# A router's last product made straight in token layout, inside a planned five-engine pipeline

## What is computed

```
x = x + layernorm(mamba(layernorm(x)))     # gated state-space block: in-projection, 4-tap causal
                                           # convolution, SiLU, softplus(delta), scan of 16 states
                                           # over 512 tokens for 512 channels, gate, out-projection
x = x + layernorm(experts(layernorm(x)))
experts(x):  Q = x WQ', K = x WK'; two branches (forward, inverse), each
   xV = Q V[k], yW = cumsum_t(K W[k]) for k in 8 experts of rank 64
   h = gelu(Q_side W1' + b1);  logits = h W2' + b2 + expert_bias;  w = softmax(logits)   # 8 logits a token
   out = sum_k (xV * yW * w[k]) U[k] + w b, over the number of tokens so far
   result = (forward + alpha inverse) WO'
```

## Time and profile before

| | us |
|---|---|
| three runs | 2418.75, 2423.53, 2423.81 |
| median | 2423.53 |
| the profiled execution | 2417.08 |
| its span, from the first to the last instruction | 2415.1 |
| VectorE busy | 2173.3 |
| TensorE busy | 2128.0 |
| GpSimd busy | 1854.3 |
| ScalarE busy | 1842.0 |
| mean granted clock of TensorE | 0.953 |

### The profile page before, as it was taken

One profiled execution on the slowest core, in us unless ns is written; L12 is line 12 of the kernel. 1 busy time (PEld: TensorE's weight loads), 2 busy tenths in 40 slices (PEclk: granted clock), 3 DMA queues, 4 the chain that ended last, 5 costly groups with the idle time before them and its releaser, 6 DMA issues.

```text
span 2415.1 us, 35863 instructions
## 1 busy us (share of the span) xinstructions
PE 2128.0 (88%) x9268; PEld 1287.7 (53%) x9268; DVE 2173.3 (90%) x2820; ACT 1842.0 (76%) x3897; POOL 1854.3 (77%) x1324
## 2 busy tenths in 40 slices
PE   5587789898998989899898989989898998988888
PEld 2355455464655546465554645555464655545454
DVE  1899999999999999999999999999998999999921
ACT  6575787869688786978778697887869788785644
POOL 3869797887879788787878878797887879787620
PEclk8797899999999999999999999999999999999999
DMA  6011110211102020111102021110202001011100
GB/s 139 31 40 41 31 49 19 67 31 59 36 28 58 18 71 28 62 32 34 52 20 68 28 62 33 30 55 23 67 27 62 31 29 56 21 60 34 31 2 16
DMA packets 83400, 101.69 MB, mean 42 GB/s; under 512 B 23480, under 2 KB 49872, under 8 KB 83168
## 3 DMA queue, kind: packets, MB, share of 16 engines
q1 hardware_dynamic: 83168, 99.06, 13.6%
HBM read 90.13 MB, written 8.91 MB: 41 GB/s over the span
## 4 chain that ended last, share of the span: by engine, by line
DVE 34%; issue 26%; PE 19%; POOL 11%; ACT 8%; DVEq 1%; DMA 1%; POOLq 0%; ACTq 0%; SPq 0%
DVE h L1347 15%; DVE yT L1363 11%; PE bank L798 10%; POOL bx L766 5%; PE stateT L971 3%; PE bank L950 3%; DVE xs L1257 2%; ACT decay L1217 2%; POOL scratch L684 1%; POOL scratch L690 1%; DVE rows L1283 1%; DVE prod L1329 1%; POOL dx L694 1%; PE bank L936 1%; DVE cumT L1303 1%
## 5 line engine op out<-in xcount | busy, mean ns | idle before, releaser
L766 POOL TENSOR_TENSOR bx<-dx,B_rows 128x1024 f32<-128x1024 f32 x512 | 1204.8, 2366 | 224.3 <-DVE h L1347 183.8
L1347 DVE TENSOR_TENSOR_SCAN h<-decay,bx 128x512 f32<-128x512 f32 x1024 | 1238.6, 1210 | 65.6 <-ACT decay L1217 54.8
L1217 ACT ACTIVATE decay<-delta,decay_rate 128x512 f32<-128x512 f32 x1024 | 703.2, 693 | 273.5 <-DVE h L1347 270.4
L971 PE MATMUL stateT<-ident,h 128*128 128x128 f32 x4096 | 640.7, 288 | 200.7 <-DVE h L1347 107.0
L971 PEld LDWEIGHTS stateT<-ident,h 128*128 128x128 f32 x4096 | 482.6, 146 | 541.1 <-issue 269.1
L1363 DVE SCALAR_TENSOR_TENSOR yT<-stateT,C_tok,yT 128x512 f32<-128x512 f32 x960 | 696.4, 726 | 24.9 <-PE stateT L971 23.8
L798 PE MATMUL bank<-k_to_expert,cumT 128*128 128x512 f32 x512 | 261.2, 635 | 6.8 <-DVE prod L1329 6.7
L798 PE MATMUL bank<-q_to_expert,xnT 128*128 128x512 f32 x512 | 249.2, 611 | 0.0
L798 PE MATMUL bank<-hT,w_in_sb 128*128 128x512 f32 x512 | 243.2, 600 | 5.5 <-DVE rows L1283 3.6
L1183 ACT ACTIVATE cum_sb<-bank,gate 128x64 f32<-128x64 f32 x1024 | 222.7, 328 | 28.7 <-PE bank L798 26.9
L950 PE MATMUL bank<-expert_to_out,prodT 128*128 128x256 f32 x1024 | 239.2, 379 | 0.0
(11 more groups left out here) (155 smaller groups left out, 2578.4 us busy)
## 6 DMA issues: line engine op xcount, KB each, us to landing
B_rows<-B_scratch SPq DMA_DIRECT2D x256, 256.0 KB, 3.2
x_front<-in_L_attn_x SPq DMA_DIRECT2D x16, 512.0 KB, 4.9
x_back<-in_L_attn_x SPq DMA_DIRECT2D x16, 512.0 KB, 4.1
out<-x_back SPq DMA_DIRECT2D x16, 512.0 KB, 4.2
w_in_sb<-in_L_attn_w_in SPq DMA_DIRECT2D x1, 1024.0 KB, 5.9
cum_sb<-in_L_ffn_V_fwd SPq DMA_DIRECT2D x2, 256.0 KB
prod<-in_L_ffn_W_inv_exp SPq DMA_DIRECT2D x2, 256.0 KB
xnT<-in_L_ffn_W_fwd SPq DMA_DIRECT2D x2, 256.0 KB
```

Of the source, the lines that this page charges most:

```text
L766: pool.tensor_tensor(bx[use % BX_RING][:, :, :], dx[q.parity][:, 2 * half:2 * half + 2, :], row, ALU.mult).then_inc(s_bx.step(f"{n},{half} ...
L971: last = pe.transpose(stateT[j % 2][:, c * P:(c + 1) * P], h[n % 2][:, c, j * P:(j + 1) * P], ident[:, :])
L1217: act.activation(decay[c % 2][:, :], delta[q.parity][:, c, :], ACT.Exp, scale=decay_rate[:, c, n:n + 1]).then_inc(s_exp.step(f"{n},{c}"), 1)
L1347: dve.tensor_tensor_scan(h[n % 2][:, c, :], decay[c % 2][:, :], bx[(2 * n + c // 2) % BX_RING][:, c % 2, :], 0.0, ALU.mult, ALU.add).then_ ...
```

## The change

The product `logit` is turned round. Each tile of 128 tokens of the hidden values becomes the stationary operand and the 8 columns of W2' the moving one, so the result has tokens on partitions: for each of 4 token tiles and 2 branches, two accumulated products of 128 x 8, all in one bank at the columns at which the transposes had put them. The copy to SBUF and the four transposes go, with their places in the plan; `lb` waits for the product itself, and the bank is free when `lb` has read it. The wait that guarded the shared place `logitT`/`gateT` moves to the copy of `gT`. There are 58 uses of banks a period, so a task now finds its bank two further on in every second period. Two tasks of TensorE (`hT`, `xnT`) get a semaphore increment where their bank's last reader is ScalarE. Nearly all other beats are new.

```
             def logit_task(b, k, use):
...
-                matmuls(use.bank[0:2 * KE, :], [(w2_padded[:, m, (1 - br) * KE:(3 - br) * KE], scratch[:, 2 * br + m, :])
-                                                for br in range(2) for m in range(DT)]).then_inc(b_pe.step("lg"), 1)
-
-            def logit_rows_task(b, k, use):
...
                 for j in range(TB):
-                    last = pe.transpose(use.bank[:, j * 2 * KE:(j + 1) * 2 * KE], logitT[:, j * P:(j + 1) * P], ident[4 * KE:6 * KE, 4 * KE:6 * KE])
-                last.then_inc(b_pe.step("lt"), 1)
+                    for br in range(2):
+                        columns = slice((2 * j + br) * KE, (2 * j + br + 1) * KE)
+                        last = matmuls(use.bank[:, columns], [(scratch[:, 2 * br + m, j * P:(j + 1) * P], w2_padded[:, m, KE:2 * KE]) for m in range(DT)])
+                last.then_inc(b_pe.step("lg"), 1)
...
-            def logit_task(b, k, use):
-                act.wait_ge(b_pe.sem, b_pe.done(b, "lg"))
-                if b.shift(-1).exists:
-                    act.wait_ge(l_pe.sem, l_pe.done(b.shift(-1), "out7"))
-                act.activation(logitT[:, :], use.bank[0:2 * KE, :], ACT.Copy).then_inc(b_act.step("lc"), 1)
...
             def gateT_task(b, k, use):
                 act.wait_ge(b_pe.sem, b_pe.done(b, "gT"))
+                if b.shift(-1).exists:
+                    act.wait_ge(l_pe.sem, l_pe.done(b.shift(-1), "out7"))
...
             def lb_task(b, k, use):
-                dve.wait_ge(b_pe.sem, b_pe.done(b, "lt"))
+                dve.wait_ge(b_pe.sem, b_pe.done(b, "lg"))
...
             def hT_task(b, t, use):
                 pe.wait_ge(f_act.sem, f_act.done(b, "h3"))
+                if use.sem is f_act.sem:
+                    pe.sem_inc(passed["pe"], 1)
```

More of the change, by code:

```diff
@@ L130 @@
[L130 to L143, removed]
@@ L158 @@
-    ("L", "cum", "act"): (356, 358, 369, 378, 390, 392, 408, 433),
[4 rows of a table removed]
-    ("L", "out", "act"): (388, 400, 442, 445),
-    ("L", "sq", "act"): (450,),
-    ("L", "rs", "pool"): (454,),
+    ("F", "sq", "act"): (2,),
+    ("F", "rs", "pool"): (16,),
+    ("F", "h", "act"): (18,),
+    ("F", "hT", "pe"): (19, 22),
+    ("F", "hT", "act"): (26, 29),
+    ("F", "x", "sp"): (112,),
+    ("F", "xs", "pe"): (32, 34, 37, 39),
+    ("F", "xs", "act"): (35, 36, 38, 42),
+    ("F", "cvA", "dve"): (34, None, 37, None),
@@ new lines @@
+    ("F", "cvB", "dve"): (35, None, 38, None),
+    ("F", "cvC", "dve"): (36, None, 39, None),
+    ("F", "tap", "act"): (None, 40, None, 42),
+    ("F", "cv", "pool"): (None, 47, None, 67),
+    ("F", "res", "pe"): (37, 40, 45, 52),
+    ("F", "res", "act"): (41, 43, 48, 56),
+    ("F", "silu", "act"): (67,),
+    ("F", "proj", "pe"): (77,),
+    ("F", "proj", "act"): (82,),
+    ("F", "B", "sp"): (85,),
+    ("F", "Ct", "pe"): (114,),
+    ("F", "Ct", "act"): (118,),
+    ("F", "dt", "pe"): (86, 90, 95, 103),
@@ new lines @@
+    ("F", "dt", "act"): (89, 94, 104, 106),
+    ("F", "ex", "act"): (90, 97, 110, 114),
+    ("F", "ln", "act"): (92, 98, 111, 117),
+    ("F", "w", "pool"): (101, 105, 115, 122),
+    ("F", "w2", "pool"): (103, 109, 116, 126),
+    ("F", "d1", "dve"): (107, 109, 123, 127),
+    ("F", "row", "sp"): (121, 123, 142),
+    ("B", "y", "pe"): (265, 266, 266, 267),
+    ("B", "u", "dve"): (264, 264, 264, 270),
+    ("B", "o", "pool"): (272, 272, 276, 277),
+    ("B", "wo", "pe"): (278, 283, 285, 286),
@@ new lines @@
+    ("B", "r", "dve"): (282, 287, 290, 291),
+    ("B", "st", "dve"): (294,),
+    ("B", "ag", "dve"): (295,),
+    ("B", "rb", "pool"): (304,),
+    ("B", "t", "act"): (303,),
+    ("B", "x1", "pool"): (309,),
+    ("B", "st1", "dve"): (305,),
+    ("B", "ag1", "dve"): (307,),
+    ("B", "rb1", "pool"): (314,),
+    ("B", "xn", "act"): (312,),
+    ("B", "xnT", "pe"): (316, 318),
+    ("B", "xnT", "act"): (320, 321),
+    ("B", "cum", "dve"): (319, 319),
+    ("B", "rt", "pe"): (321, 322, 327, 329),
@@ new lines @@
+    ("B", "rt", "act"): (326, 330, 332, 332),
+    ("B", "gelu", "act"): (336,),
+    ("B", "logit", "pe"): (339,),
+    ("B", "lb", "dve"): (339,),
+    ("B", "mx", "dve"): (340,),
+    ("B", "sub", "pool"): (348,),
+    ("B", "ex", "act"): (344,),
+    ("B", "sm", "dve"): (343,),
+    ("B", "sn", "pool"): (356,),
+    ("B", "rc", "dve"): (347,),
+    ("B", "wa", "pool"): (357,),
+    ("B", "gT", "pe"): (363,),
+    ("B", "gT", "act"): (368,),
+    ("L", "cum", "pe"): (347, 358, 366, 375, 382, 390, 402, 433),
@@ L166 @@
+    ("L", "xv", "pe"): (353, 362, 366, 378, 395, 427, 430, 434),
+    ("L", "cum", "act"): (357, 360, 370, 378, 392, 392, 410, 438),
[4 rows of a table added]
+    ("L", "out", "act"): (389, 400, 446, 455),
+    ("L", "sq", "act"): (456,),
+    ("L", "rs", "pool"): (474,),
     ("L", "t", "act"): (468,),
-    ("F", "dx", "pool"): (108, 109, 127, 131),
-    ("L", "x", "pool"): (476, 479),
-    ("L", "store", "sp"): (471,),
+    ("F", "dx", "pool"): (112, 114, 127, 128),
+    ("L", "x", "pool"): (477, 479),
+    ("L", "store", "sp"): (456,),
```

68 lines of the change are left out of this document (8 added, 60 removed), and 10 rows, old and new, of tables (FILLED_BY, TIMETABLE).

## The result

The changed kernel takes 2489.25 us (median of 4 runs, 2484.03 to 2489.95), the kernel before 2423.4 beside it: ratio 1.0272, 95% interval 1.0253 to 1.029. It is 66 us slower; I had forecast 2422 and a range up to 2440.

The account below looks back on a forecast made before the run. VectorE was taken to set the pace, busy 90% of the span. The terms +1.5 (bias add), -1.8 (dips), -1.8 (first period), +0.8 (end) sum to -1.3 us: 2422 from the median 2423.5; range 2405 to 2440, to hold 8 in 10.

Parts of the forecast that it names:

- The price of the block: TensorE's new logit product, 32 weight loads and matmuls of 8 columns: 3.7 us, with bounds of 1.9 and 6.9.
- Rival C: The new logit block keeps TensorE's clock at 1.2 GHz behind it, doubling dt0 and cum0: +15 us, 2437; chance 0.10.
- The wait of the bias add: On VectorE, lb at the product's own beat 339 waits 0.1 us for it in 15 batches: +1.5 us.
- Rival B: The logit block is longer than lb's place allows, from 3.6 us on: 2436 at 0.14 us a pair; chance 0.20.
- My sign of B: A stall of lb for TensorE above 0.2 us a batch would show the block too long for lb's place.
- that of C: Granted clock under 0.97 in steady batches would show that the block keeps the clock down.
- Clock dips: Stretches at 1.2 GHz: spreading work of beats 103 to 106 gives -8.8, new block +5, other dips +2; together -1.8 us.
- Stalls at Silu and Gelu: VectorE's two stalls a batch for the decay tile, 1.66 and 1.80 us, were to stay: 3.46 us kept.
- The thin margins: Waits with little slack at r0, cum, st1, pr7 and dx3: all 0, or 0 to 0.3 us a batch.
- ScalarE's copy: Removing one copy of 0.59 us a batch from ScalarE, 9.4 us in all, gains 0 in the steady part.
- The first period: At the scan at 85.70 us, one more decay tile is out before ScalarE's h waits for rstd: -1.8 us.
- The end: After the last scan: the product gains 1.3 us, out6 and out7 ahead of the router cost 2.1: sum +0.8.

Follow-up runs that it names:

- e3: The changed kernel with each small product streaming its 8 columns 16 times (N = 128); 2454.16 us, ratio to the kernel before 1.01 to 1.0165.
- after: The changed kernel itself, new beats and product of 8 columns, against the kernel before; 2489.25 us, ratio 1.0253 to 1.029.
- e1: The kernel before on its old beats, with the new product of 8 columns in place of the old product, copy and transposes; 2470.28 us.
- e4: The kernel before on its old beats, with the new product widened to N = 128; 2425.03 us, ratio 1.0001 to 1.003.
- e12: The kernel before with the new product at 8 columns and the fourth dt product moved from beat 106 to 110; 2436.56 us.
- e11: The kernel before with the new product at N = 128 and the fourth dt product moved from beat 106 to 110, run again; 2408.01 us.
- e8: The changed kernel with the bias add moved from beat 339 to 342 and the router's softmax on its old beats; 2488.98 us.
- e2: The changed kernel's new beats with the old product, copy and transposes, the router's end on its old beats; 2450.89 us.
- e10: The kernel before with only the fourth dt product moved from beat 106 to 110; 2411.69 us, ratio 0.9938 to 0.997.
- e7: The changed kernel with each small product streaming its 8 columns 4 times (N = 32); 2481.87 us, ratio to the kernel before 1.0228 to 1.0289.

## Why the prediction was wrong, by its steps

**The price of the block: right.** 3.7 us forecast, 3.73 measured at full clock. The 0.11 us between two full weight loads was the right row to go by. The Trainium skill's rule on overlap ("TensorE: Matmul & The Clock Gate", Part 3), by which the block would have taken 13 us by my estimate, is contradicted here. e3 shows it best: 512 columns took 3.61 / 8 = 0.45 us, so 128 take 0.11 by estimate, as long as a load; one after the other 32 pairs would take 7 us, and they took 3.83.

**Rival C: the mechanism that came true, and the failed step.** The sum held nothing for the clock behind the block; I gave that 0.10 and 15 us. I had argued that transposes in every second beat left a steady batch at 0.99, so small products would too. But those stream 128 columns each, and the rows before held no product of 8; one does not bound the other. The 0.99 was also one stretch read as the mean, which is 0.97. Widening alone gives back 35 us on the new beats (after, e3), 45 on the old (e1, e4) and 28 on the relieved ones (e12, e11), so that is its price. It was also mis-sized: I let dt0 and cum0 double, 1 us a batch. The stretch lasts up to 17.1 us, dt1 and the transposes are slow in it, and the block too, to 5.8 us in the steady part, so its own cost doesn't stay at 3.7.

The Trainium skill ("TensorE: Matmul & The Clock Gate", Part 4) says that transposes do not count as busy for the gate in the way products do. The runs here show plain products under which the clock falls at N = 8 and 32, and the same loads under which it doesn't at 128; they do not set transposes apart.

**The wait of the bias add, +1.5: right in kind, and beside the point.** In e3, with the block at full clock, the logits' waits are 24.1 us with one of 19.3 after the last scan, 4.8 in 13 batches, 0.4 each. In the changed kernel it became 21 us, and e8 shows that moving the add away brings nothing. I let Rival B decide from 3.6 us of block length; a late queue is paid at the next reader, wherever the first one stands. My sign of B (more than 0.2 us a batch at the bias add) came true with that of C (a granted clock under 0.97), so the signs did not tell the two apart; e1 and e8 did.

**Clock dips, -1.8: the wrong sign, +29 to +30.** e2, and e3 against e4, give the beats' price. The gap at 103 to 106 was read rightly (e10 gets 10 us by relieving it, my 8.8), but I looked for new heavy gaps by equal beats (37, 110, 122) and missed the neighbours 90 and 91, which fall between the same two groups of transposes, in the very stretch where the clock falls. Parting them is worth 16 of the 30 us.

**Stalls at Silu and Gelu, 3.46 us kept: 1.47 and 1.22.** Both smaller, with 0.47 behind the projection at beat 77 in their place, which I had not counted.

**The thin margins, 0: held.** Between 480 and 2160 us VectorE waits at none of r0, cum, st1, pr7 and d1. But the pairs about beat 122, of which I had thought only in a dip, do stall: in e3 yT waits 0.93 and 0.94 us at 621.75 and 626.94, and behind the scan of beat 124 9.5 us in 12 batches. ScalarE's copy was worth 0, as said: ScalarE waits for VectorE 388.5 us, more than before.

**The first period, -1.8: wrong.** The decay tile was early, but a job of the weights waited and the transposes stood behind it. TensorE and VectorE of the changed kernel:

```profile
84.50 3.78 PE L790 MATMUL bank<-cum_sb,rows 128*128 128x512 f32 x4 [3.32 <-ACT gate L991]
88.08 1.06 PE L965 MATMUL stateT<-ident,h 128*128 128x128 f32 x4
```

```profile
89.18 0.75 DVE L1353 SCALAR_TENSOR_TENSOR yT<-stateT,C_tok,yT 128x512 f32<-128x512 f32 x1 [5.62 <-PE stateT L965]
```

The scan that had waited 2.44 us gave place to a wait of 5.62. The jobs' beats follow from the table; I had left them out. From the first scan of batch 0 to that of batch 1 the profiled execution takes 4.3 us more than that of the kernel before. e2 and e3 have the same wait (5.6 us), so it belongs to the beats.

**The end, +0.8: it was +5.3.** So much longer is the time from the last scan's end to the last instruction, in the one profiled execution of each kernel. From the router's first product to the bias add:

```profile
2407.20 7.13 PE L795 MATMUL bank<-xnT,q_to_router 128*128 128x512 f32 x16
2418.51 6.97 PE L795 MATMUL bank<-w_padded,scratch 128*128 128x8 f32 x32 [4.17 <-ACT scratch L1149]
```

The block ran to 2425.48, 7.0 us where I had 5.2, all at the lower clock. out6 and out7 stood ahead as said, and the router's first product started 3.4 us later behind the last scan than before, where I had 2.1. That puts the bias add 3.9 us later; the last 1.3 us come behind it.

**The sum.** The period grew from 140.4 to 144.8 us, 52 us in the 12 periods measured. The profiled executions differ by 72 us, a little more than the medians; the rest is 9.8 us in the first three periods, 5.2 in the last, 5.3 at the end, and 0.8 less before the first scan. As medians the 66 us are made of 50 (the narrow product, e1) and 30 (the beats, e2), less 14 for which I have only an argument: the two meet in one stretch of late work.

## What to carry to other kernels

Before a product is turned so that a thin operand moves, ask what TensorE's clock does behind it: here 32 full weight loads with 8 columns each left the neighbours at 1.2 GHz, and reading the same 8 columns 16 times in a product cost 0.1 us a block and gave 28 to 45 us back. In a pipeline with a planned order, look at what stands *between* two pieces that the critical engine waits for, not at equal times; take the sum of it at the lower clock, and compare it with what the critical engine has in hand. A wait that vanishes when its reader is moved, with the total unchanged, was a place of payment, not a cause.

## What the runs showed of the hardware that I had not expected

- A busy TensorE can lose its clock: 5.59 of 5.60 us busy, and 0.64 granted; in the 17.1 us from 728.0 on, all busy, 0.51. What differs from e3's 1.00 is only that each product streams 8 columns and not 128. The runs vary nothing else, and do not say by what measure the clock goes.
- Between 8, 32 and 128 columns the block's length hardly moves at full clock (3.73, 3.75, 3.83 us for 32), while the time at 1.2 GHz goes 423, 402, 294 us (after, e7, e3).
- A weight load and a small product of all 128 rows take 0.117 us together (3.73 / 32), against 0.11 from load to load. With 128 columns the pair takes 0.120 us (3.83 / 32), though load and product would each take 0.11 alone (the product's by the estimate above): the product lies beside the next load, and both use all 128 rows.
